# Score and maximum matmuls as two 64-row tiles, and the weighted sums of both halves of a step together

## What is computed

```
Q, K, V = split_heads(query @ Wq + bq), split_heads(key @ Wk + bk), split_heads(value @ Wv + bv)   # 16 heads of 8
scores  = einsum('bhqd,bhkd->bhqk', Q, K) / sqrt(8)          # 4 x 16 x 256 x 1601
attn    = softmax(scores)
ctx     = einsum('bhqk,bhkd->bhqd', attn, V)
x       = x + ctx @ Wo + bo
```

## Time and profile before

| | |
|---|---|
| median of 3 runs | 507.23 us (506.89 to 507.24) |
| profiled execution, span from first to last instruction | 502.5 us |
| what lies around the span, against the median | 4.7 us |
| TensorE matmul busy | 447.6 us (89%) |
| VectorE busy | 351.7 us (70%) |
| ScalarE busy | 299.8 us (60%) |
| granted TensorE clock, mean | 0.929 |

### The profile page before, as it was taken

The page is one execution under the profiler, slowest core; times in us unless marked ns, Lnnn a source line. Parts: engine busy times, 40 slices in busy tenths (PEclk is TensorE's granted clock), DMA queues, the critical chain, the costliest instruction groups (busy, mean ns, idle before and its releaser), DMA issues.

```text
span 502.5 us, 10204 instructions
## 1 busy us (share of the span) xinstructions
PE 447.6 (89%) x3264; PEld 197.8 (39%) x3264; DVE 351.7 (70%) x829; ACT 299.8 (60%) x608; POOL 58.1 (12%) x55
## 2 busy tenths in 40 slices
PE   1755899999899998999999997999999999999956
PEld 1542133445333434455333334455333435333224
DVE  3773988885969784786978882876878886892041
ACT  1411057676576756586677746586677648778811
POOL 3500000370000000460000000460000000000000
PEclk9856579999999999999999999999999999999956
DMA  6064720042032201051141202051140200000000
GB/s 223 3 223 127 207 90 2 1 149 99 27 117 70 74 5 47 34 191 57 31 142 39 77 1 82 1 198 50 33 151 30 77 1 12 1 2 0 1 0 12
DMA packets 18884, 33.80 MB, mean 67 GB/s; under 512 B 1424, under 2 KB 16400, under 8 KB 18832
## 3 DMA queue, kind: packets, MB, share of 16 engines
q1 hardware_dynamic: 18832, 33.10, 20.1%
HBM read 17.33 MB, written 11.93 MB: 58 GB/s over the span
## 4 chain that ended last, share of the span: by engine, by line
PE 68%; DVE 16%; issue 6%; DMA 5%; ACT 3%; SPq 1%; POOL 1%; DVEq 0%; POOLq 0%; ACTq 0%
PE wsum L976 18%; PE score L994 17%; PE ring L1010 15%; DVE part_max L634 8%; DMA q_unit<-q_rows 2%; PE ring L1145 2%; PE ring L1114 2%; PE ring L1107 2%; PE ring L1053 2%; DMA q_rows<-q_parts 2%; PE ring L1043 2%; PE ring L1021 1%; PE ring L1150 1%; PE ring L1157 1%; PE ring L1137 1%
## 5 line engine op out<-in xcount | busy, mean ns | idle before, releaser
L634 DVE TENSOR_REDUCE part_max<-ring 128x1 f32<-128x401 f32 x512 | 260.6, 567 | 81.4 <-PE ring L1010 80.2
L848 ACT ACTIVATE probs<-score 128x512 f32<-128x512 f32 (+1 forms) x416 | 224.8, 598 | 71.4 <-PE score L994 70.1
L1010 PE MATMUL ring<-k_unit,q_unit 96*128 96x401 bf16 x512 | 143.1, 355 | 7.2 <-DMA q_unit<-q_rows 6.3
L994 PE MATMUL score<-q_unit,k_unit 128*128 128x512 bf16 (+1 forms) x416 | 128.6, 390 | 5.4 <-issue 5.0
L976 PE MATMUL wsum<-probs,v_unit 128*32 128x256 f32 (+1 forms) x1664 | 130.6, 391 | 0.6 <-ACT q_unit L859 0.6
L1010 PEld LDWEIGHTS ring<-k_unit,q_unit 96*128 96x128 bf16 x512 | 48.6, 100 | 96.4 <-issue 25.5
L976 PEld LDWEIGHTS wsum<-probs,v_unit 128*32 128x32 f32 (+1 forms) x1664 | 34.2, 108 | 64.5 <-issue 42.0
L994 PEld LDWEIGHTS score<-q_unit,k_unit 128*128 128x128 bf16 (+1 forms) x416 | 31.6, 100 | 68.1 <-ACT probs L848 49.2
L859 ACT ACTIVATE q_unit<-ring 3x1024 bf16<-3x1024 bf16 x16 | 16.3, 1017 | 31.4 <-PE ring L1021 30.9
L595 POOL TENSOR_TENSOR var<-mv,c_sb 128x2 f32<-128x2 f32 x4 | 0.8, 197 | 228.7 <-DVE mv L784 228.7
L563 POOL TENSOR_TENSOR k_parts<-k_full,c_sb 128x802 bf16<-128x802 f32 x7 | 10.7, 1524 | 132.9 <-ACT k_full L894 132.9
(11 more groups left out here) (105 smaller groups left out, 316.0 us busy)
## 6 DMA issues: line engine op xcount, KB each, us to landing
k_unit<-k_rows SPq DMA_DIRECT2D x32, 300.2 KB
v_unit<-v_aug SPq DMA_DIRECT2D x16, 234.0 KB, 5.7
ctx_sb<-ctx_t SPq DMA_DIRECT2D x4, 800.5 KB, 6.3
k_rows<-k_parts SPq DMA_DIRECT2D x4, 601.5 KB, 3.3
k_rows<-k_parts SPq DMA_DIRECT2D x4, 599.2 KB, 3.7
k_rows<-k_parts SPq DMA_DIRECT2D x4, 401.0 KB, 4.1
k_rows<-k_parts SPq DMA_DIRECT2D x4, 399.5 KB, 4.3
q_unit<-q_rows SPq DMA_DIRECT2D x32, 48.0 KB
```

The source lines that it names most:

```text
L634: v_.tensor_reduce(part_max[:, par, q, head, hp, c:c + 1], ring[s][:, 0:CW], AX.X, ALU.max)\
L848: a_.activation(probs[0:rows, i % PB, :], score[i % EB][0:rows, :], ACT.Exp)\
L994: mm(score[i % EB][0:keys, :], k_unit[:, u, L * hp + P * t:L * hp + P * t + keys], q_unit[:, u, :, hp, :], start=True, stop=True).then_inc ...
L1010: mm(ring[s][:, 0:CW], q_unit[0:PR, mu, par, hp, P * q:P * (q + 1)], k_unit[0:PR, mu, L * hp + (CW - 1) * c:L * hp + (CW - 1) * c + CW], s ...
```

## The change

Each head block gets a 64-row half of the array of its own: k_unit and q_unit hold rows 0 to 50 and 64 to 114, three rows for ones and maxima first (`MR`) and 48 of the head behind them (`KR` = 51). q_unit has no zero blocks any more. A score half is four matmuls of 256 columns, two per bank, and waits once for the later of its two banks. A maximum item is two matmuls, one on each half, into two ring slots, and two reductions; `MU`, `AHEAD` and `QUOTA` are halved to match. The plan of a step is now: score half 0, one item of maxima, score half 1, one item, side items of the middle, the weighted sums of both halves, the rest. The ones come by two DMAs from the constants at the start, and zeros for the three rows of q_unit by two more DMAs with each load of queries; the memsets are gone. The maximum's copy on ScalarE is two instructions.

```diff
-MU = 4 * QT * KC
-AHEAD = (4, 8, 8, 8)
+MU = 2 * QT * KC
+AHEAD = (2, 4, 4, 4)
...
-QUOTA = [[5, 5, 5, 5, 4, 4, 4], [5, 5, 5, 5, 4, 4, 4], [6, 6, 6, 4, 2, 0, 4], [7, 7, 6, 6, 2, 4, 4]]
+QUOTA = [[3, 2, 3, 2, 2, 2, 2], [3, 2, 3, 2, 2, 2, 2], [3, 3, 3, 2, 1, 0, 2], [4, 3, 3, 3, 1, 2, 2]]
...
-                plan += todo[:2]
-                todo = todo[2:]
-            if half == 1:
-                if step == 1 and prev:
-                    plan.append(("norm", "norm"))
-                side(step, "mid")
-            if step:
-                plan.append(("PV", step - 1, half))
-            elif prev and half == 0:
+                plan += todo[:1]
+                todo = todo[1:]
+            if step == 0 and prev and half == 0:
                 plan.append(("PVlast",))
+        if step == 1 and prev:
+            plan.append(("norm", "norm"))
+        side(step, "mid")
+        if step:
+            plan.append(("PV", step - 1, 0))
+            plan.append(("PV", step - 1, 1))
...
-        q_unit = sb("q_unit", [P, UB, 2, 2, S], BF16)
+        q_unit = sb("q_unit", [P, UB, 2, S], BF16)
...
+            for par in range(2):
+                ones = consts[0:MR, C_COLS["ones"][0]:C_COLS["ones"][1]]
+                sp.dma_start(k_unit[HALF * par:HALF * par + MR, :, :].bitcast(F32),
+                             ones.unsqueeze(1).to_broadcast([MR, UB, L])).then_inc(ones_in, 16)
...
+                    sp.dma_start(q_unit[HALF * par:HALF * par + MR, u, :, :].rearrange("p h n -> p (h n)").bitcast(F32),
+                                 consts[0:MR, C_COLS["zeros"][0]:C_COLS["zeros"][1]]).then_inc(unit_in[u], 16)
...
-            def set_unit(u):
-                v_.memset(k_unit[PR:P, u, :].bitcast(F32), TWO_ONES)
-                v_.memset(q_unit[:, u, :, :, :].rearrange("p a h n -> p (a h n)").bitcast(F32), 0.0)\
-                    .then_inc(unit_set, 1)
...
-                    s, n = take("M")
-                    v_.tensor_reduce(part_max[:, par, q, head, hp, c:c + 1], ring[s][:, 0:CW], AX.X, ALU.max)\
-                        .then_inc(drained[s], 1)
+                    for head in range(2):
+                        s, n = take(f"M{head}")
+                        v_.tensor_reduce(part_max[:, par, q, head, hp, c:c + 1], ring[s][:, 0:CW], AX.X, ALU.max)\
+                            .then_inc(drained[s], 1)
...
-                    a_.activation(q_unit[PR:PR + 3, mu, :, :, :].rearrange("p a h n -> p (a h n)"),
-                                  ring[s][PR:PR + 3, :].bitcast(BF16), ACT.Copy).then_inc(drained[s], 1)
+                    for par in range(2):
+                        rows = slice(HALF * par, HALF * par + MR)
+                        last = a_.activation(q_unit[rows, mu, :, :].rearrange("p h n -> p (h n)"),
+                                             ring[s][rows, 0:S].bitcast(BF16), ACT.Copy)
+                    last.then_inc(drained[s], 1)
...
-                    for hp in range(2):
-                        i = GU * u + 2 * t + hp
-                        free = bank_free_count(b, i)
-                        if free is not None:
-                            pe.wait_ge(probs_done, free)
-                        mm(score[i % EB][0:keys, :], k_unit[:, u, L * hp + P * t:L * hp + P * t + keys],
-                           q_unit[:, u, :, hp, :],
-                           start=True, stop=True).then_inc(scores_ready, 1)
+                    i = GU * u + 2 * t
+                    free = bank_free_count(b, i + 1)
+                    if free is not None:
+                        pe.wait_ge(probs_done, free)
+                    for hp in range(2):
+                        for par in range(2):
+                            rows = slice(HALF * par, HALF * par + KR)
+                            last = mm(score[(i + par) % EB][0:keys, S * hp:S * (hp + 1)],
+                                      k_unit[rows, u, L * hp + P * t:L * hp + P * t + keys], q_unit[rows, u, hp, :],
+                                      start=True, stop=True)
+                            if hp == 1:
+                                last.then_inc(scores_ready, 1)
...
-                    mm(ring[s][:, 0:CW], q_unit[0:PR, mu, par, hp, P * q:P * (q + 1)],
-                       k_unit[0:PR, mu, L * hp + (CW - 1) * c:L * hp + (CW - 1) * c + CW], start=True, stop=True)\
-                        .then_inc(filled[s], 1)
+                    slots = [take(f"M{par}")[0] for par in range(2)]
+                    for par in range(2):
+                        rows = slice(HALF * par, HALF * par + KR)
+                        mm(ring[slots[par]][:, 0:CW], q_unit[rows, mu, hp, P * q:P * (q + 1)],
+                           k_unit[rows, mu, L * hp + (CW - 1) * c:L * hp + (CW - 1) * c + CW], start=True, stop=True)\
+                            .then_inc(filled[slots[par]], 1)
```

More of the change, by code:

```diff
@@ L50 @@
 TR = TERMS * DX
-PR = 2 * TR
+MR = 3
+KR = MR + TR
+HALF = P // 2
 VW = DX + 1
 VQ = 4 * VW
-TWO_ONES = float(np.array([0x3F803F80], np.uint32).view(np.float32)[0])
+TWO_ONES = np.array([0x3F803F80], np.uint32).view(np.float32)[0]
 VPAD = KT * VQ + 32 - VW
@@ L73 @@
                         ("cos", 2 * S), ("sin", 2 * S), ("mask", 3 * P),
-                        ("select", 16), ("blocks", 4)])
+                        ("select", 16), ("blocks", 4), ("ones", L), ("zeros", S)])
 W_FIRST = W_COLS["Wv"][1]
 C_FIRST = C_COLS["zero"][1]
+C_HELD = C_COLS["blocks"][1]
 def constants():
@@ L106, in constants @@
     put("blocks", np.eye(4, dtype=np.float32))
+    put("ones", np.full((MR, L), TWO_ONES, np.float32))
     return c
@@ L190, in unit_plan @@
     return plan
-SET_AFTER = ("ln1", "e1", "av", "ln2")
 NO_SLOT = ("ln1", "ln2", "ln3", "soft", "store0", "store1", "load")
 def ring_uses(plan):
-    return sum(1 for item in plan if item[0] in ("M", "mT", "norm", "prep", "post") and item[1] not in NO_SLOT)
+    return sum(2 if item[0] == "M" else 1
+               for item in plan if item[0] in ("M", "mT", "norm", "prep", "post") and item[1] not in NO_SLOT)
 START_PLAN = ([("prep", name) for name in PREP_ALL] + [("M", "M", 1, k) for k in range(MU)] + [("mT", "mT")] +
@@ L452, in wait_unit_free @@
             def wait_unit_free(b, u):
-                if isinstance(b, int) and b == 0:
-                    sp.wait_ge(unit_set, u + 1)
-                else:
+                if not (isinstance(b, int) and b == 0):
                     sp.wait_ge(pv_done, STEPS * (UB * (b - 1) + u + 1))
@@ L489, in do @@
                 kind = item[0]
-                if kind in ("M", "norm", "mT", "prep", "post") and item[1] not in NO_SLOT:
+                if kind == "M":
+                    clock.take("M0")
+                    clock.take("M1")
+                elif kind in ("norm", "mT", "prep", "post") and item[1] not in NO_SLOT:
                     clock.take(item[1])
@@ L858, in do @@
                     s, n = take("mT")
-                    a_.activation(q_unit[PR:PR + 3, mu, :, :, :].rearrange("p a h n -> p (a h n)"),
-                                  ring[s][PR:PR + 3, :].bitcast(BF16), ACT.Copy).then_inc(drained[s], 1)
-                elif kind in ("M", "norm"):
-                    clock.take(item[1])
+                    for par in range(2):
[3 more added lines that the diff above has]
+                    last.then_inc(drained[s], 1)
+                elif kind == "M":
+                    clock.take("M0")
+                    clock.take("M1")
+                elif kind == "norm":
+                    clock.take("norm")
                 elif kind == "prep":
@@ L974, in products @@
                 for j in range(4):
-                    i = GU * u + 2 * t + j // 2
+                    i = GU * u + 2 * t + j % 2
                     last = mm(wsum[32 * j:32 * j + 32, 0:S], v_unit[0:rows, u, VQ * t + VW * j:VQ * t + VW * j + 32],
-                              probs[0:rows, i % PB, S * (j % 2):S * (j % 2 + 1)], start=t == 0, stop=t == KT - 1)
+                              probs[0:rows, i % PB, S * (j // 2):S * (j // 2 + 1)], start=t == 0, stop=t == KT - 1)
                 if half == 1 or t == KT - 1:
@@ L1019, in do @@
                             for q in range(QT):
-                                at = S * (2 * par + hp) + P * q
-                                last = turn(ring[s][PR:PR + 3, :].bitcast(BF16)[:, at:at + P],
+                                at = S * hp + P * q
+                                last = turn(ring[s][HALF * par:HALF * par + MR, :].bitcast(BF16)[:, at:at + P],
                                             max_parts[:, 4 * q + 2 * par + hp, :], ident_bf[:, :])
```

20 lines of the change are left out of this document (9 added, 11 removed).

## The result

The changed kernel takes 557.24 us (median of 4 runs, 554.83 to 562.83); the kernel before, on the same chip, 507.06. The ratio is 1.109 (95% interval 1.102 to 1.117). The forecast was 498 us, 1.8% faster: it has the wrong sign, and 557 lies outside its range of 482 to 530. The profiled execution has a span of 560.9 us against 502.5.

The account below looks back on a forecast made before the run. TensorE was taken to bound most units, VectorE the one at 255.4, ScalarE the last. The order saves 17.6 us, clock drops lose 9, leaving 9 less: 502.5 - 9 + 4.7 = 498 us, range 482 to 530.

Parts of the forecast that it names:

- the clock term: TensorE's clock in the loop: extra drops to 1.2 GHz over three rounds, costing 9 us in all.
- The number of drops: Two more clock drops a round: one in the stretch from 237.2, one in the feed-forward.
- The price of one: One clock drop lasts 4 us and loses 1.5 us, priced by a quiet step at 1.2 GHz.
- the thinnest stretch of before: Stretch from 237.2, TensorE at full clock waiting for VectorE; the clock was expected to fall there.
- the clock stays low: Rival, chance 0.30: after a drop TensorE's clock stays low, 17 steps a round; 558 us, or 524 with half of that.
- Tiles overlap: Score and maximum matmuls on two 64-row tiles run together: score half 0.22 for 0.44, maxima pair 0.175 for 0.35 us.
- Weight loads take the room: Rival, chance 0.05: four serial loads of 0.10 make a score half 0.40 us; +22, about 517 us.
- Entry and exit of the weighted sums: Steps 1 to 5 each save one entry (0.09) and exit (0.14) of the 32-column arrangement, 0.23 us.
- The bank wait: Steps 1 to 5: second score half waits for the first's exponential, starting 1.07 us after it, TensorE idle 0.68.
- The saving of the order, 17.6: Gains and losses of all units and the start, before the clock loss: 17.6 us less.
- The query wait: Unit at 232.1: next round's first maxima wait for queries, 0.65 us late before, stall 1.8 to 2.0 after; gain 0.

Follow-up runs that it names:

- the first filler's version: Changed kernel plus two purposeless 512-column matmuls before the score-bank wait of the second score half in steps 1 to 5; 517.08 us, ratio 1.026.
- the version with all fillers and early zeros: Changed kernel plus 512-column filler before second score halves and the x2T and x3T layernorm waits, query zero rows loaded with the keys; 506.97 us, ratio 1.012.
- the merge alone: Kernel before, with only the weighted sums of both halves of a step put together, scores and maxima on all rows; 503.9 us, ratio 1.001.
- the tiles alone: Changed kernel with the old step order, each half's weighted sums following its maxima, 64-row tiles kept; 520.19 us, ratio 1.025.
- The four-bank version: Changed kernel with four score banks in place of three and three ring slots for maxima in place of four; 584.51 us, ratio 1.149.
- the tiny filler: Changed kernel plus two 4-column matmuls before the score-bank wait of each second score half in steps 1 to 5; 542.51 us, ratio 1.081.

## Why the prediction was wrong

**The step that failed** is the clock term: "I take two more such drops a round, 4 us long each, 1.5 lost: 3 x 2 x 1.5 = 9." It measures about 49. I take each unit of the changed kernel less the same unit at the full clock in a version with the merge and filler, where the filler lies in holes; the pauses at the loop's turn are taken out everywhere (us):

| unit of a round | before | changed | same order, full clock |
|---|---|---|---|
| from 213.7, projections | 33.75 | 37.57 | 33.63 |
| from 255.8 | 23.36 | 26.14 | 23.17 |
| from 282.0 | 21.70 | 23.13 | 20.89 |
| from 305.1, feed-forward | 30.55 | 35.08 | 30.84 |
| last unit, to the end of its normalisation matmuls | 16.68 | 25.67 | 18.29 |

The last column is from the first filler's version for the unit from 255.8 and the last one, and from the version with all fillers and early zeros for the others. In this way all 16 units together take 405.5, 452.0 and 403.1 us: the clock costs 48.9, the order of the work saves 2.4. The very first unit ran at the full clock in no version; it stands in the 403.1 with 20.6 us at a clock of 0.82 (21.6 at 0.71 in the changed kernel), so both figures are a little too small. The two turns of the loop stand 15.2 us in place of 5.0, the first unit starts 0.9 later, and 0.7 more lie behind the last one: 48.9 - 2.4 + 10.2 + 0.9 + 0.7 = 58.3, the difference of the two spans.

- *The number of drops.* Both that I expected are there (the step at 237.2 of before; step 5 of the feed-forward, 9.9 us for 5.9). Not foreseen: the unit from 282.0, step 1 of the feed-forward, the loop's turn, and the last unit, low from its second step to the end.
- *The price of one.* I put 1.5. The drop of the unit from 255.8 costs 2.9 (6.44 and 5.63 for 5.66 and 3.48), that in the feed-forward about 4. I had priced it by a quiet step; where side work stands in the step, all of it is at half speed.
- *What I read wrongly.* I looked for the thinnest stretch of before, and took one place. But the change takes half of scores and maxima out of every stretch that is paced by VectorE or ScalarE, all at once. Wherever a step's length doesn't shrink, TensorE's share of it does.

**The rival "the clock stays low"** (0.30) gave 558, and 557.2 was measured; that is luck in part, since its mechanism isn't what happened in the round. It wanted one low stretch of 17 steps; there are five, 48 us of a round of 129, some 8 steps, dearer each, and the loop's pauses. In the last unit it is right to the letter: with a bank wait in each step the clock stays at 0.5 and a step is 3.76 for 2.46 at full.

**Point by point, the other steps:**
- *Tiles overlap.* Right. A score half is 0.23 (put: 0.22), a pair of maxima 0.26 before weighted sums (0.175 + 0.09), 0.18 before scores.
- *Weight loads take the room* (rival): wrong. Four loads of mean 100 ns go into a half of 0.23. The Trainium skill (TensorE: Matmul & The Clock Gate, LDWEIGHTS) gives a load of 128 columns 107 ns; the duration agrees, and the loads lie beside other matmuls.
- *Entry and exit of the weighted sums.* 0.10 to 0.16 a step with the merge alone, 0.23 put.
- *The bank wait.* Right in place and size: hole 0.57 (0.68), second half 1.14 after the first (1.07), quiet step 2.82 and 2.69 (2.72 and 2.55). I took it for a matter of three banks; it is the merge that uncovers it, as the tiles alone show. The four-bank version could not settle it for whole units, since it starves the ring; its last unit, 2.6 us shorter, fits.
- *The saving of the order, 17.6.* It measures 2.4. At the full clock: quiet unit 1.2 (2.5), unit from 255.8 0.2 (0), from 282.0 0.8 (1.1), feed-forward 0.3 longer (2.2 shorter), last unit 1.6 longer (0.7). The projections were to gain 0.7 and cost 1.4 in the first such unit (34.1 for 32.71): in the changed kernel a second half there waits 0.65 for ScalarE, with eight 256-column matmuls and the weighted sums behind it.
- *The query wait.* It grew from 0.65 to 1.38, by 0.7 and not 2; loading the zeros early brings it back to 0.54 and gives no time that could be measured.
- *The loop's turn.* Not in the prediction at all, and 10 of the 58 us. The pauses change with the instructions in the loop's body, and each ends behind the landing of an instruction packet. Why the changed kernel has two at a turn, and why the packet of the second sets out only at 216.28, 2.2 us into it, stays open; the load of 800 KB that SP issues at 212.24 is a rival that no run tests. Open too is why the tiny filler, with next to no work, spares drops of the clock elsewhere (its unit from 123.0 is 23.3 us at 1.00, the changed kernel's 26.1 at 0.80).

That the clock is the cause and not only a companion is shown by the pair of fillers: same instructions, same waits, same pauses at the loop's turn, 512 or 4 columns, 517 or 542 us. The pair shows 25 of the 49 us; the rest rests on the units' lengths in the table.

## What to carry to other kernels

A change that makes TensorE's work shorter where another engine sets the pace buys no time there and lowers TensorE's activity; work out for each stretch how busy TensorE will be after it, and count the loss at half speed over everything in that stretch, side work too. Change one part at a time: of the two here the tiles save 2.9 us a quiet unit and the merge gives back 1.7, by taking away the work that covered a bank wait. Matmuls with no purpose, put exactly into waits, can pay (542 us with 4 columns each, 517 with 512), and cost nearly in full where nothing waits (505 to 520). When two versions are compared, take the pauses at the loop's turn out first: here they part versions by up to 12 us, and they are not what the idea under test is about.

## What the runs showed that I had not expected

- A clock that fell where TensorE had no hole over 1.28 us, and stayed at 0.50 for 8.8 us in which it was busy 8.45.
- Adding work made a kernel 40 us faster, about 12 of them in pauses at the loop's turn.
- Pauses at the loop's turn of 1.5 to 8.1 us, in kernels that differ in a few dozen instructions, each ended 1.1 to 2.4 us after an instruction packet of 16 KB had landed.
